# Gate folded into the output weights, and three tiles' residual rows added on TensorE in a fused attention and feed-forward kernel

## The reference, cut to what matters

```python
# x: 2 x 1024 x 256, context: 2 x 77 x 256, 8 heads of 64
x = x + tanh(g_xattn[0]) * attention(layernorm(x), context, Wq, Wk, Wv, Wo, bo)
x = x + tanh(g_ffn[0]) * ffn(layernorm(x), w1, b1, w2, b2)
# attention: q = ln(x) Wq; k, v = context Wk, context Wv; softmax(q k^T / 8) v, then @ Wo + bo
# ffn: inputs, weights and biases rounded to 8-bit fixed point, relu between the two layers
```

## Time and profile before

| | us |
|---|---|
| runs of the kernel | 123.6, 124.03, 125.75 |
| median | 124.03 |
| the profiled execution's own time | 123.75 |
| its span | 122.0 |
| PE busy / PEld busy / DVE busy | 115.0 / 104.9 / 97.3 |
| ACT busy / POOL busy | 77.2 / 87.3 |
| granted TensorE clock | full speed in every slice |

### The profile page before, as it was taken

How to read it: one execution, slowest core, us unless ns; L and a number is a source line. 1 busy time by engine, 2 the same in 40 slices (tenths; PEclk the granted TensorE clock), 3 DMA queues, 4 the chain that set the end, 5 groups by cost and what they waited for, 6 DMA issues and landing times.

```text
span 122.0 us, 2891 instructions
## 1 busy us (share of the span) xinstructions
PE 115.0 (94%) x1013; PEld 104.9 (86%) x1013; DVE 97.3 (80%) x219; ACT 77.2 (63%) x168; POOL 87.3 (72%) x160
## 2 busy tenths in 40 slices
PE   7899995999999989999999999999999999999990
PEld 2589974999797989999999999999999997987880
DVE  2009789799999999899999999989797969437981
ACT  4168682968769895995757484848482919347420
POOL 3003757689498989899888949894989495996620
PEclk9999999999999999999999999999999999999999
DMA  2989799300000000000020002000200020020104
GB/s 73 340 236 370 254 371 377 145 0 5 3 0 3 8 0 0 0 0 5 0 86 5 0 0 86 0 3 5 86 0 0 3 91 0 0 86 8 65 21 172
DMA packets 5312, 8.87 MB, mean 73 GB/s; under 512 B 1175, under 2 KB 2226, under 8 KB 5170
## 3 DMA queue, kind: packets, MB, share of 16 engines
q1 hardware_dynamic: 5210, 8.61, 19.9%
q10 hardware_dynamic: 88, 0.08, 0.2%
HBM read 6.59 MB, written 2.10 MB: 71 GB/s over the span
## 4 chain that ended last, share of the span: by engine, by line
PE 61%; DVE 17%; ACT 8%; POOL 4%; issue 4%; DMA 3%; SPq 0%; ACTq 0%; DVEq 0%; POOLq 0%
PE of_ps L815 18%; PE sc_ps L782 13%; PE h_ps L842 9%; PE of_ps L857 7%; PE tr_ps L794 5%; DVE probs L573 3%; DMA wk_sb<-in_L_xattn_Wk_dram 3%; DVE mx L568 3%; DVE den L580 2%; ACT probs L403 2%; PE tr_ps L718 2%; ACT pT L430 2%; PE tr_ps L764 2%; DVE pT L609 1%; PE tr_ps L857 1%
## 5 line engine op out<-in xcount | busy, mean ns | idle before, releaser
L815 PE MATMUL of_ps<-u_sb,pT 128*128 128x256 f32 x240 | 31.1, 281 | 0.9 <-ACT x2T L450 0.8
L782 PE MATMUL sc_ps<-a_sb,xT 128*128 128x308 f32 x192 | 31.2, 311 | 0.7 <-DVE probs L573 0.7
L815 PEld LDWEIGHTS of_ps<-u_sb,pT 128*128 128x128 f32 x240 | 29.5, 188 | 1.9 <-issue 1.9
L403 ACT ACTIVATE probs<-probs,rstd 128x616 f32<-128x616 f32 x16 | 13.1, 816 | 26.1 <-DVE probs L573 25.8
L782 PEld LDWEIGHTS sc_ps<-a_sb,xT 128*128 128x128 f32 x192 | 27.5, 189 | 1.5 <-issue 1.3
L444 ACT ACTIVATE hid_q<-h_ps,b1z 128x256 int8<-128x256 f32 x58 | 24.7, 491 | 3.9 <-PE h_ps L842 3.9
L282 POOL TENSOR_TENSOR probs<-probs,rden 128x616 f32<-128x616 f32 x16 | 19.5, 1221 | 1.5 <-DVE rden L583 1.5
L331 POOL CAST hid<-hid_q 128x512 bf16<-128x512 int8 x27 | 15.8, 611 | 2.0 <-ACT hid_q L444 2.0
L842 PE MATMUL h_ps<-x2T,w1T 128*128 128x256 bf16 x128 | 16.6, 273 | 0.0
L568 DVE TENSOR_REDUCE mx<-sc_ps 128x8 f32<-128x616 f32 x16 | 12.6, 790 | 4.2 <-PE sc_ps L782 4.2
L842 PEld LDWEIGHTS h_ps<-x2T,w1T 128*128 128x128 bf16 x128 | 12.4, 98 | 1.6 <-ACT x2T L450 0.3
(11 more groups left out here) (113 smaller groups left out, 176.9 us busy)
## 6 DMA issues: line engine op xcount, KB each, us to landing
w_sb<-in_L_ffn_w_dram SPq DMA_DIRECT2D x2, 1024.0 KB, 11.1
out_dram<-x_sb SPq DMA_DIRECT2D x7, 256.0 KB, 2.5
x_sb<-in_x_dram SPq DMA_DIRECT2D x4, 256.0 KB, 8.1
x_sb<-in_x_dram SPq DMA_DIRECT2D x1, 1024.0 KB, 10.0
wk_sb<-in_L_xattn_Wk_dram SPq DMA_DIRECT2D x1, 512.0 KB, 4.0
wq_sb<-in_L_xattn_Wq_dram SPq DMA_DIRECT2D x1, 512.0 KB, 5.0
wv_sb<-in_L_xattn_Wv_dram SPq DMA_DIRECT2D x1, 512.0 KB, 7.8
wo_sb<-in_L_xattn_Wo_dram SPq DMA_DIRECT2D x1, 512.0 KB, 8.8
```

The source lines that it names most:

```text
L403: nc.scalar.activation(probs_v(T), probs_v(T), ACT.Exp, scale=rstd1[:, T:T + 1]).then_inc(exp_done, 1)
L782: ins = nc.tensor.matmul(sc_ps[:, a, 0:HALF], xT[:, T % 2, p, c, :], a_sb[:, q, T // TB, c, HALF * a:HALF * a + HALF], start=first, stop=last)
L815: ins = nc.tensor.matmul(attn_ps, pT[:, T % 2, p, P * c:P * c + P], u_sb[:, q, MC * (T // TB) + c, :], start=first, stop=last)
```

## The change

`u_copy` and `u1_copy` multiply by the gate on ACT as they copy, and DVE's `u_low` becomes a multiply and subtract; the bias row is gated once on ACT (`bo_gated`). With U gated, the attention output in PSUM is already what is added to x. For tiles 2 and 4 to 15 DVE adds the two with a plain `tensor_tensor`. For tiles 0, 1 and 3 (`SUMMED`) TensorE multiplies the tile's rows of `x_sb` by the identity into the same PSUM tile ahead of the 15 matmuls, and ACT copies the sum out (`rows_summed`). DVE has no instruction for these three residuals. The two loads of the gates go from SP's queue to the head of ACT's, behind one load of the context, and the tanh stands earlier on ACT.

```diff
+SUMMED = (0, 1, 3)
 ...
-            sp.dma_start(g_sb[:, 0:1], g_xattn.rearrange("(a n) -> a n", a=1).to_broadcast([P, 1])).then_inc(g_in, 16)
-            sp.dma_start(g_sb[:, 1:2], g_ffn.rearrange("(a n) -> a n", a=1).to_broadcast([P, 1])).then_inc(g_in, 16)
 ...
             def u_copy(b, n):
                 act.wait_ge(u_psum, 3 * b + n + 1)
-                nc.scalar.copy(u_of(b, n, 0), u_banks[b, n]).then_inc(u_high, 1)
+                nc.scalar.activation(u_of(b, n, 0), u_banks[b, n], ACT.Identity, scale=tg[:, 0:1]).then_inc(u_high, 1)
 ...
+            def rows_summed(T):
+                act.wait_ge(attn_psum, T + 1)
+                nc.scalar.copy(x_sb[:, T, :], attn_ps).then_inc(x1_ready, 1)
 ...
             act.dma_start(ctx_sb[:, 1, :], ctx_in[1, :, :]).then_inc(ctx_in_sb, 16)
+            act.dma_start(g_sb[:, 0:1], g_xattn.rearrange("(a n) -> a n", a=1).to_broadcast([P, 1])).then_inc(g_in, 16)
+            act.dma_start(g_sb[:, 1:2], g_ffn.rearrange("(a n) -> a n", a=1).to_broadcast([P, 1])).then_inc(g_in, 16)
 ...
             for s in range(TILES):
                 if live(s + 1):
                     exponentials(s + 1)
+                if s - 1 in SUMMED:
+                    rows_summed(s - 1)
                 pT_copy(s)
 ...
             def u_low(b, n):
                 dve.wait_ge(u_high, 3 * b + n + 1)
-                nc.vector.tensor_tensor(u_of(b, n, 1), u_banks[b, n], u_of(b, n, 0).bitcast(F32), ALU.subtract).then_inc(u_ready, 1)
+                nc.vector.scalar_tensor_tensor(out=u_of(b, n, 1), in0=u_banks[b, n], scalar=tg[:, 0:1], in1=u_of(b, n, 0).bitcast(F32),
+                                               op0=ALU.mult, op1=ALU.subtract).then_inc(u_ready, 1)
 ...
-                nc.vector.scalar_tensor_tensor(out=x_sb[:, T, :], in0=attn_ps, scalar=tg[:, 0:1], in1=x_sb[:, T, :],
-                                               op0=ALU.mult, op1=ALU.add).then_inc(x1_ready, 1)
+                nc.vector.tensor_tensor(x_sb[:, T, :], attn_ps, x_sb[:, T, :], ALU.add).then_inc(x1_ready, 1)
 ...
                 if live(s - 1):
-                    residual(s - 1)
+                    if s - 1 not in SUMMED:
+                        residual(s - 1)
                     stats_second(s - 1)
 ...
             def attend(T):
-                pe.wait_ge(pT_high, T + 1)
                 if T > 0:
                     pe.wait_ge(x1_ready, T)
                 if T > 1:
                     pe.wait_ge(x2T_ready, T - 1)
+                if T in SUMMED:
+                    pe.wait_ge(x_in[min(T, TB) // 2], 16)
+                    nc.tensor.matmul(attn_ps, ident[:, :], x_sb[:, T, :], start=True, stop=False)
+                pe.wait_ge(pT_high, T + 1)
```

More of the change, by code:

```diff
@@ L78, in flamingo_kernel @@
         bo_sb = sb("bo_sb", [1, D])
+        bo_gated = sb("bo_gated", [1, D])
         g_sb = sb("g_sb", [P, 2])
@@ L312, in bias_rows @@
             def bias_rows():
-                pool.wait_ge(bo_in, 16)
+                pool.wait_ge(bo_high, 1)
                 pool.wait_ge(u_ready, 1)
-                nc.gpsimd.tensor_copy(u_sb[0:1, 0, 0, :], bo_sb[:, :]).then_inc(bo_high, 1)
-                pool.wait_ge(bo_high, 1)
-                nc.gpsimd.tensor_tensor(u_sb[0:1, 1, 0, :], bo_sb[:, :], u_sb[0:1, 0, 0, :].bitcast(F32),
+                nc.gpsimd.tensor_copy(u_sb[0:1, 0, 0, :], bo_gated[:, :]).then_inc(bo_high, 1)
+                pool.wait_ge(bo_high, 2)
+                nc.gpsimd.tensor_tensor(u_sb[0:1, 1, 0, :], bo_gated[:, :], u_sb[0:1, 0, 0, :].bitcast(F32),
                                         ALU.subtract).then_inc(bo_rows, 1)
@@ L421, in u1_copy @@
                 act.wait_ge(u_psum, 4 + n)
-                nc.scalar.copy(u1_whole[:, n, :], u_banks[1, n]).then_inc(u1_copied, 1)
+                nc.scalar.activation(u1_whole[:, n, :], u_banks[1, n], ACT.Identity, scale=tg[:, 0:1]).then_inc(u1_copied, 1)
             def u_copy(b, n):
                 act.wait_ge(u_psum, 3 * b + n + 1)
-                nc.scalar.copy(u_of(b, n, 0), u_banks[b, n]).then_inc(u_high, 1)
+                nc.scalar.activation(u_of(b, n, 0), u_banks[b, n], ACT.Identity, scale=tg[:, 0:1]).then_inc(u_high, 1)
             def pT_copy(T):
@@ L494, in _ @@
             a1_copy(3)
+            act.wait_ge(g_in, 32)
+            nc.scalar.activation(tg[:, :], g_sb[:, :], ACT.Tanh).then_inc(tg_ready, 1)
             act.wait_ge(vz_zero, 1)
@@ L503, in _ @@
             xT_copy(2)
+            act.wait_ge(tg_ready, 1)
             u_copy(0, 0)
@@ L507, in _ @@
             minus_centred(4)
-            act.wait_ge(g_in, 32)
-            nc.scalar.activation(tg[:, :], g_sb[:, :], ACT.Tanh).then_inc(tg_ready, 1)
+            act.wait_ge(bo_in, 16)
+            nc.scalar.activation(bo_gated[:, :], bo_sb[:, :], ACT.Identity, scale=tg[0:1, 0:1]).then_inc(bo_high, 1)
             for s in range(TILES):
@@ L813, in attend @@
                     for c in range(MC):
-                        first, last = (c, p, q) == (0, *PARTS[0]), (c, p, q) == (MC - 1, *PARTS[-1])
+                        first = (c, p, q) == (0, *PARTS[0]) and T not in SUMMED
+                        last = (c, p, q) == (MC - 1, *PARTS[-1])
                         ins = nc.tensor.matmul(attn_ps, pT[:, T % 2, p, P * c:P * c + P], u_sb[:, q, MC * (T // TB) + c, :],
```

## The result

The change is slower: 127.53 us (127.28 to 128.35, 6 runs) against 124.08 us, a ratio of 1.031 with a 95% interval of 1.0285 to 1.0334. The profiled execution took 127.6 us with a span of 125.7, so it is 3.85 us above the profiled one of before, where 2.0 were forecast. It lies outside the range of 123.7 to 127.0.

What follows compares the result with a forecast made beforehand. It took DVE to pace the early steps, with a hand-over in steps 3 and 4, then PE without a wait from 50.78 us; 123.75 + 1.79 for the steps + 0.2 for the loads gave 125.8 us, range 123.7 to 127.0.

Steps and rivals of the forecast that it cites:

- The sign: Whole kernel: the change makes it slower, +1.4% against the median.
- the moved loads: Kernel start: gate loads travelling beside Wk cost 0.2 us, with bounds of 0 and about 1 us.
- Steps 1 and 2: Tiles 0 and 1: ACT's copy queues behind the exponential, so DVE's statistics start 0.80 us later in each.
- Folding the gate in: Two u_low on DVE's chain cost +0.14 us together; residuals on a chain in step 3 and at the end, -0.07 each.
- Step 3: Attention of tile 3: added matmul exposed behind the x2T wait at 0.46 us; PE's attention moves by +1.9 to +2.2.
- The slack: Step 3: ACT's late exponential, for which DVE waits 0.16 us, can swallow 0 to 0.30 us of the delay.
- Steps 4 and 5, and PE's run: Attention of tile 4 at +1.79 us, tile 5 at +1.86; PE's run then keeps that, +1.79 with the last residual.
- Step 5: Attention of tile 5: starts 0.11 us after tile 3's x2T copy, at 52.64, which is +1.86 us.
- The second rival: Kernel start: gate loads hold Wk back beyond about 6.0, up to 1 us more, 126.9 us; chance 0.14.
- The first rival: Steps 1, 2 and 4: DVE does not wait for the copies, but PE cannot follow; 124.1 us, chance 0.14.

Runs made afterwards that it cites:

- e4: The change with gate loads back on SP's queue and ACT's copy of the summed rows ahead of the exponential: 124.26 us against 123.9 before.
- e7: The change with gate loads back on SP's queue and no tile summed, so only the fold is left: 123.43 us against 123.86 before.
- e1: The kernel before with only the two gate loads moved to ACT's queue behind the context half: 125.7 us against 123.9 before.
- e10: The kernel before with only the first gate's load moved to ACT's queue behind the context half: 126.88 us, ratio 1.0082.
- e11: The kernel before with both gate loads on ACT's queue behind the copy of ctxT: 123.65 us against 123.79 before.
- e6: The kernel before with both gate loads in SP's queue between the first context half and Wk: 128.35 us against 123.86 before.
- e9: The change with one edit, ACT's copy of the summed rows ahead of the exponential, gate loads still early: 126.36 us against 123.79 before.
- e2: The change with the gate loads back on SP's queue and the tanh just ahead of the first exponential: 125.72 us against 123.9 before.

## Why the prediction missed the size

The sign was right and the time, 127.5 against 125.8, was outside the range. The step that failed is the term of the moved loads, put at 0.2 us and measured at 1.8 to 2.0. Point by point:

- **Steps 1 and 2** (+0.80 each for DVE): measured +0.77 a step, idle time 1.19 for 1.2. Shown by the timeline, and by e4, where moving the copy by one place on ACT takes the whole of it back.
- **Folding the gate in**: two u_low at +0.14 together; measured 1.27 against 1.15 on the chain, +0.12. Residuals at 424 ns for 415. e7, the fold alone, is 0.4 us under before, where the forecast had it at nothing. The traces show some 0.15 of that as the fold's, and DVE's subtractions no earlier, so the cause of the whole is open.
- **Step 3**: the added matmul exposed at 0.46; measured: from the first of its records at 42.38 to the end of the 15 at 44.81 there are 2.43 us where 2.00 were needed, +0.43. The size was right, the path was not. The matmul was forecast behind the wait for ACT's x2T copy; in the trace TensorE last waits (0.41 us) for DVE's residual of tile 2, and from 40.33 on goes through the scores into the added matmul without a wait. The slack of 0.16 to 0.30 us, read from the late exponential in the earlier trace rows, is the gap that e1, e10 and e11 do not have: one execution was taken for the rule.
- **Steps 4 and 5, and PE's run**: +1.79 without the loads. The last residual is 3.78 later, of which the start before the steps holds 2.00 (8.75 to 10.75): 1.78. That it fits to 0.01 is partly luck. On the way the attention of tile 4 is at +1.57 (forecast 1.79), that of tile 5 at +1.66 (1.86) and that of tile 6 at +1.90. Step 5 was working with 0.11 us from the end of an x2T copy to the attention, where the earlier trace rows have 0.14 and 0.15.
- **The moved loads**: this is the step that failed. The prediction took 0.2 us for them, with 0 and 1 as bounds; e1 has 1.8 in time, and the trace of the change 2.00. The low value rested on first loads that leave engine time free. The windows of before do not have it: the DMA share is 0.98 and 0.96 from 4 to 6 us. The upper bound was read from windows at 12 to 14 us, where the two landed before and the rate was down by a third, while at the head it fell to 144 and 117 GB/s, by 0.6, with TensorE waiting for the very next load. It also counted a delay of Wk alone, and Wq, 2.7 us late, was waited for last. There was a better row for the size: before, the second gate landed at 15.4 us, 2.5 behind the first, and in the change it is again 2.5 (6.65 and 9.15), in e6 2.3.
- **The second rival** had this mechanism, its place and its condition (Wk later than 6.0), at a chance of 0.14; its price of 1.0 was half of what came.
- **The rule of the Trainium skill** (DMA: Bandwidth & Descriptors, section Queues, rings and completion order), that a DMA engine takes turns between queues, is in agreement with e1, where Wq on SP's queue is 2.7 us late beside two loads on ACT's. It was the warning against the small number. e6 shows that it is not needed for the harm.
- **The first rival** (DVE freed, TensorE in its place, 124.1) did not happen in the change, but e4, with the copy ahead and the gates late, is that case, at 124.26. A gain of 2% had no room, as said.

## What to carry to other kernels

When work is moved from a busy engine to an idle one, look at what stands ahead of it in that engine's queue: here the idle time of ACT lay in front of the exponential and the copy was put behind it, which made a 0.4 us saving a 0.8 us loss, and one place earlier DVE keeps 0.34 us of the saving. Ask too who is next: DVE's load was replaced by matmuls on TensorE, and that was the engine with the least room. And do not move loads of many tiny elements in front of or beside the loads that the first matmuls wait for; one instruction later, behind the first copy, the same two cost nothing. Last, check a gap of 0.3 us that one trace shows against a second trace before it enters a sum.

## What the runs showed of the hardware

- Two loads of 128 elements of 4 bytes each, issued beside Wk and Wq, made Wq land 2.7 us late (e1, the change), one made it 1.3 us late (e10); with the two in front of Wk in the same queue, the DMA engines moved 27 and 53 GB/s for two microseconds (e6). The second of two such loads landed 2.3 to 2.7 us behind the first in before, the change, e1, e6 and e11, though issued only 0.4 us behind it.
- A plain float32 matmul of 128x256 costs TensorE 0.43 us in a stream of others (two records), where the same columns in the attention product take 0.12 (15 in 1.76).
- TensorE's granted clock fell to 0.5 about 1 us into the key matmuls of one execution (e9), which had followed a wait of 1.79 us; in others (e10, e2) the same slowness came with a recorded clock of 1.00, after waits of 1.64 and 0.49 us, and after a wait of 1.83 us (the change) it did not come at all.
